# Local block: the inverse roots for q and k made by VectorE with a product of two quadratics, in place of ten small operations of GpSimd

## What is computed

```python
def l2norm(t):
    return t / jnp.maximum(jnp.linalg.norm(t, axis=-1, keepdims=True), 1e-12)

def attn_layer(x, Wqkv, qs, ksc, Wo):          # 16 heads of 64, window of 32
    q, k, v = jnp.split(x @ Wqkv, 3, -1)       # then by heads
    q = l2norm(q) * qs
    k = l2norm(k) * ksc
    q = q * cos * scale + rotate_half(q) * sin * scale
    k = k * cos / scale + rotate_half(k) * sin / scale
    return local_attention(q, k, v) @ Wo

for i in range(6):
    x = attn_layer(shift_tokens(x), ...) + x
    x = ffn_layer(shift_tokens(x), ...) + x
```

## Time and profile before

| | before |
|---|---|
| median of 3 runs | 4272.27 us (4267.4 to 4280.25) |
| profiled execution | 4279.95 us, span 4278.2 us |
| mean granted TensorE clock | 0.971 |
| TensorE (PE) busy | 3950.0 us, 92% |
| weight loads (PEld) busy | 2888.7 us, 68% |
| VectorE (DVE) busy | 3287.6 us, 77% |
| ScalarE (ACT) busy | 2637.3 us, 62% |
| GpSimd (POOL) busy | 2977.4 us, 70% |

### The profile page before, as it was taken

The page is one execution under the profiler, slowest core; times in us unless marked ns, Lnnn a source line. Parts: engine busy times, 40 slices in busy tenths (PEclk is TensorE's granted clock), DMA queues, the critical chain, the costliest instruction groups (busy, mean ns, idle before and its releaser), DMA issues. The chain is left out here.

```text
span 4278.2 us, 151283 instructions
## 1 busy us (share of the span) xinstructions
PE 3950.0 (92%) x66376; PEld 2888.7 (68%) x66376; DVE 3287.6 (77%) x4155; ACT 2637.3 (62%) x3184; POOL 2977.4 (70%) x3649
## 2 busy tenths in 40 slices
PE   8999969999999999999878887799999999999997
PEld 5655657777777777777633333577777777777775
DVE  4535568888888888888668884688888888888885
ACT  4424436667767666666537774367667767667664
POOL 2202158889888888888634440788888988888884
PEclk9999989999999999999979998899999999999998
DMA  4304332333233323322100000332333333233221
GB/s 152 126 10 141 110 92 79 80 94 84 79 87 86 86 76 87 88 69 73 40 11 1 1 1 1 110 84 78 87 79 86 89 82 89 74 87 84 75 68 37
DMA packets 169727, 316.93 MB, mean 74 GB/s; under 512 B 39336, under 2 KB 43056, under 8 KB 166640
## 3 DMA queue, kind: packets, MB, share of 16 engines
q1 hardware_dynamic: 153520, 241.18, 20.8%
q0 software_dynamic: 15552, 66.07, 5.0%
HBM read 92.03 MB, written 20.05 MB: 26 GB/s over the span
## 5 line engine op out<-in xcount | busy, mean ns | idle before, releaser
L695 PE MATMUL psum<-loc_w_hl,loc_z_lo 128*128 128x512 f32 x1152 | 513.9, 446 | 39.5 <-DMA loc_w_hl<-parted 26.0
L1191 DVE TENSOR_REDUCE loc_ssq<-loc_sq 128x16 f32<-128x1024 f32 x384 | 464.6, 1210 | 24.2 <-POOL loc_rn L1074 24.2
L936 ACT ACTIVATE loc_sq<-psum 128x1024 f32<-128x1024 f32 x192 | 196.5, 1024 | 457.1 <-PE psum L697 452.0
L1078 POOL TENSOR_TENSOR loc_rc_k<-loc_rc_k,loc_rs_k 128x1024 f32<-128x1024 f32 x192 | 454.1, 2365 | 18.7 <-DVE loc_rs_k L1205 18.7
L1078 POOL TENSOR_TENSOR loc_rc_q<-loc_rc_q,loc_rs_q 128x1024 f32<-128x1024 f32 x192 | 459.1, 2391 | 0.0
L696 PE MATMUL psum<-loc_w_hl,loc_z_hi 128*128 128x512 f32 x1152 | 455.8, 396 | 2.1 <-issue 2.1
L1186 DVE TENSOR_TENSOR loc_rc_q<-psum,loc_rot 128x1024 f32<-128x1024 f32 x192 | 235.0, 1224 | 289.1 <-ACT loc_sq L931 159.9
L697 PE MATMUL psum<-loc_w_hl,loc_z_hi 128*128 128x512 f32 x1152 | 455.7, 396 | 0.2 <-issue 0.2
L792 PE MATMUL psum<-loc_PT,loc_V 64*64 64x32 f32 x24576 | 405.1, 220 | 7.3 <-issue 6.7
L792 PEld LDWEIGHTS psum<-loc_PT,loc_V 64*64 64x64 f32 x24576 | 381.2, 135 | 33.7 <-issue 10.1
L1097 POOL TENSOR_TENSOR loc_prob<-loc_prob,loc_recip 128x1024 f32<-128x1024 f32 x192 | 365.4, 1903 | 43.6 <-DVE loc_recip L1228 43.5
(11 more groups left out here) (198 smaller groups left out, 9616.7 us busy)
## 6 DMA issues: line engine op xcount, KB each, us to landing
loc_V<-loc_V SPq DMA_DIRECT2D x1152, 128.0 KB
loc_V<-loc_V SPq DMA_DIRECT2D x672, 64.0 KB
loc_w_hl<-parted POOLq DMA_DIRECT2D x72, 512.0 KB, 4.4
parted<-moe_halves POOLq DMA_DIRECT2D x18, 1024.0 KB, 5.2
moe_spread<-moe_gates SPq DMA_DIRECT2D x64, 256.0 KB, 4.0
moe_raw<-in_wqkv POOLq DMA_DIRECT2D x18, 512.0 KB, 6.3
moe_w<-in_moe_w SPq DMA_DIRECT2D x32, 256.0 KB, 3.3
loc_wo<-in_wo SPq DMA_DIRECT2D x12, 512.0 KB, 5.1
```

The costliest lines, as they stand in the source:

```text
L695: pe.matmul(M.bank[bank + g], z_lo[:, r, tokens], w[:, 0, cols], start=True, stop=False)
L1078: pool.tensor_tensor(rc, rc, rs[:, :], ALU.add).then_inc(added, 1)
L1191: dve.tensor_reduce(ssq[:, a:a + HEADS], heads(sq[:, :]), AX_X, ALU.add).then_inc(totalled, 1)
```

## The change

The function `root` moves from GpSimd's list to VectorE's, behind `guess`, and becomes six operations in five dependent stages: t = g*g*x, with g the guess and x the sum of squares, and then g times the product of two quadratics in t. The leading factor of that product goes into the tables of cosine and sine. The guess goes to a tensor `rg` of its own, so that `rn` is written once. `floored` becomes a `scalar_tensor_tensor` with `ssq` as both inputs.

```diff
+ROOT_LEAD = 0.27406619329149995
+ROOT_FACTORS = ((-0.9034896806386632, 1.7067896912217941), (-4.2420135386446685, 5.265389317482745))
...
-            def root(L, t):
-
-                step = L * (TS * 9) + t * 9
-                pool.wait_ge(guess_ready, upto(L, t))
...
-                pool.tensor_tensor(rn[:, :], rn[:, :], rt[:, :], ALU.mult).then_inc(root_ready, 1)
-
...
             def step(L, n, live):
-                if live(n - 1):
-                    root(L, n - 1)
...
-                dve.tensor_scalar(ssq[:, :], ssq[:, :], 1e-24, None, ALU.max).then_inc(floor_ready, 1)
+                dve.scalar_tensor_tensor(out=ssq[:, :], in0=ssq[:, :], scalar=1e-24, in1=ssq[:, :], op0=ALU.max,
+                                         op1=ALU.max).then_inc(floor_ready, 1)
...
-                dve.tensor_scalar(rn[:, :].bitcast(I32), ssq[:, :].bitcast(I32), -0.5, float(0x5F3759DF), ALU.mult,
+                dve.tensor_scalar(rg[:, :].bitcast(I32), ssq[:, :].bitcast(I32), -0.5, float(0x5F3759DF), ALU.mult,
                                   ALU.add).then_inc(guess_ready, 1)
+
+            def root(L, t):
+
+                step = (L * TS + t) * 5
+                (a, b), (c, d) = ROOT_FACTORS
+                dve.wait_ge(guess_ready, upto(L, t))
+                dve.tensor_tensor(rt[:, :], rg[:, :], rg[:, :], ALU.mult).then_inc(root_step, 1)
+                dve.wait_ge(root_step, step + 1)
+                dve.tensor_tensor(rt[:, :], rt[:, :], ssq[:, :], ALU.mult).then_inc(root_step, 1)
+                dve.wait_ge(root_step, step + 2)
+                dve.scalar_tensor_tensor(out=rv[:, :], in0=rt[:, :], scalar=c, in1=rt[:, :], op0=ALU.add,
+                                         op1=ALU.mult).then_inc(root_step, 1)
+                dve.scalar_tensor_tensor(out=ru[:, :], in0=rt[:, :], scalar=a, in1=rt[:, :], op0=ALU.add,
+                                         op1=ALU.mult).then_inc(root_step, 1)
+                dve.wait_ge(root_step, step + 3)
+                dve.scalar_tensor_tensor(out=rv[:, :], in0=rv[:, :], scalar=d, in1=rg[:, :], op0=ALU.add,
+                                         op1=ALU.mult).then_inc(root_step, 1)
+                dve.wait_ge(root_step, step + 5)
+                dve.scalar_tensor_tensor(out=rn[:, :], in0=ru[:, :], scalar=b, in1=rv[:, :], op0=ALU.add,
+                                         op1=ALU.mult).then_inc(root_ready, 1)
...
                 if live(n):
                     floored(L, n)
                     guess(L, n)
+                    root(L, n)
...
-    tab = np.stack(tabs).astype(f)
+    tab = (np.stack(tabs) * ROOT_LEAD).astype(f)
```

More of the change, by code:

```diff
@@ L557, in local_transformer_block @@
         rc_k = sb("rc_k", [P, 2, INNER])
-        ssq, rn, rt, ru = (sb(n, [P, 2 * HEADS]) for n in ("ssq", "rn", "rt", "ru"))
+        ssq, rn, rg, rt, ru, rv = (sb(n, [P, 2 * HEADS]) for n in ("ssq", "rn", "rg", "rt", "ru", "rv"))
         qk_q, qk_k = (sb(n, [P, PAIRS, 2, DH]) for n in ("qk_q", "qk_k"))
```

## The result

The changed kernel takes 4345.12 us (median, 4326.52 to 4353.02) beside 4275.96 us (4267.4 to 4280.25) for the kernel before on the same chip: a ratio of 1.015, 95% interval 1.0123 to 1.0178. The change costs 1.5%, about 65 us. The forecast was 4253 us with a range up to 4315: wrong in its sign, and the time is outside the range.

A forecast was written before the change was run, and what follows sets the result against it. GpSimd's loop was taken as the bound, 63.3 us per four-tile group. New loop: 58.5 + 1.54 + 0.7 + 1.0 + 0.9 + 0.3 = 62.9; 0.4 x 48 = 19 us off the 4272 median gives 4253, range 4195 to 4315.

The forecast's parts named there:

- The stall moves: Local block: a VectorE-GpSimd-VectorE loop of 14.63 us per plain tile replaces GpSimd's; DMA issues fall into its waits, costing nothing.
- sum of 62.9 us per group: New loop over four local-block tiles plus extras, against 63.3 before; TensorE's 60.8 us busy time stays under it.
- rival (c): Nothing happens, 4272 us: small steps eat the 0.4 us, or TensorE and the awaited squares already set the pace; chance 0.24.
- without a hole: VectorE runs from the q sine product to the reciprocal's end with no wait, 9.03 us per tile.
- new loop: Plain local-block tile: VectorE to the reciprocal, GpSimd's normalise and add k, then VectorE's floor, guess and root; 14.63 us.
- The floor: VectorE's small instruction before the guess: held by GpSimd's add k for 1.8 us, mean rising from 886 ns to 1.5 or more.
- rival (b): Faster by more: only tensor_scalar waits for GpSimd, the new instruction forms don't; 72 us gained, 4200 us; chance 0.12.
- The root: Inverse root on VectorE, five dependent stages at 194 ns plus 0.03 each: 1.12 us per tile, bounds 0.9 to 1.25.
- The deviation chain: GpSimd's eight small instructions, every fourth tile: their 1.04 us power catches the third or fourth root step, costing 0.9 us.
- rival (a): Slower: the deviation chain wins shared access at every root step, root 1.2 us later every fourth tile, 4310 us; chance 0.22.
- z_lo: GpSimd instruction slipping in ahead of the guess: guess takes about 1 us every fourth tile, adding 1.0 us per group.
- The reciprocal: GpSimd's normalise waits for VectorE's reciprocal about 2.7 us in nearly every tile, 300 to 500 us in all.

The follow-up runs named there:

- e8: Changed kernel with the weight DMA issue moved behind scale q in GpSimd's list: 4279.42 us, 0.9995 of the kernel before.
- e16: e8 plus six useless 128x32 products on GpSimd behind the root: 4332.58 us, ratio 1.0122 to the kernel before.
- e7: Changed kernel with the weight issue waiting for VectorE's root, plus six useless 128x32 GpSimd products ahead of that issue: 4289.59 us, ratio 1.0024.
- e12: e8 with the six root operations on VectorE left out: 4249.59 us, 0.9931 of the kernel before.
- e10: Changed kernel with the weight issue moved behind normalise, ahead of add k: 4408.83 us, ratio 1.0304 to the kernel before.

## Why the prediction was wrong, and where it was right

**The step that failed** stands under "The stall moves": the DMA issues "fall into the new waits (1.8 us before the floor, 2.7 us before normalise), so they cost nothing while those waits stand". For the 0.6 us of GpSimd's time this is true: in the example the issue at 1511.57 lies in a wait of GpSimd for the root (a third wait, neither of the two named). But I had priced only the instruction, not its transfer, and not that GpSimd's list without the root lets it go 3.7 us earlier. SyncE's queue was never looked at. The price of that step was 66 us (after against e8); its term in the sum was nought. No rival had it.

**The loop was not the bound.** The sum of 62.9 us per group (the additions redone give the same but for 0.1 us of table factors) stood on the claim that "TensorE's 60.8 us stay under 62.9", with idle time left as it was. Without the collision, e8, the waits of TensorE over the stretch are

```profile
PE psum L768 <- issue: 33.8, 26, 2.4
PE psum L794 <- issue: 6.8, 11, 1.3
PE psum L697 <- issue: 4.9, 4, 1.9
PE psum L824 <- DVE loc_gg L1247: 4.8, 8, 0.9
```

The wait for q is gone, 30.5 us, and the waits for issue, all lines together, went from 17.7 us to 48.8. Wait for q and waits for issue together are 48.2 us before and 48.8 in e8: the relief was taken back by TensorE's own stalls, and a group takes 64.4 us there, not 62.9. So the 19 us of forecast gain were not there even with the collision away: 4279 against the 4253 forecast. That is rival (c), by its second reason (TensorE already near its pace); I had given it 0.24. The likely reading is that while TensorE waited for q its instruction supply caught up, and that this wait had hidden the stalls. That is argued from the equal sums; e16, meant to test it, was spoiled by its overlap, and e7 can't test it, for TensorE has no wait for q there. It stays open. TensorE is not the bound alone: leaving six operations off VectorE gave 30 us (e12).

**VectorE "without a hole"** was wrong. The waits of VectorE in the changed kernel, same stretch:

```profile
DVE loc_rc_q L1159 <- ACT loc_sq L933: 105.2, 79, 7.1
```

It waits for ScalarE's square of q in 79 of 80 tiles, 1.3 us on average (70.3 us at 58 places before). ScalarE in turn waits for TensorE's projections, mostly ahead of the square of k, which comes earlier in its list:

```profile
ACT loc_sq L938 <- PE psum L699: 206.9, 79, 6.0
ACT loc_sq L933 <- PE psum L699: 21.8, 22, 2.1
```

So the new loop goes through TensorE too. The prediction had seen that wait and dismissed it, because the floor behind it waited for GpSimd anyway; when that cover went, it should have been put in. It also explains the next point.

**The floor** was to rise from 886 ns to 1.5 us or more. It fell:

```profile
L1169 DVE SCALAR_TENSOR_TENSOR loc_ssq<-loc_ssq 128x32 f32<-128x32 f32 x79 | 43.3, 548 | 4.8 <-DVE loc_ssq L1164 0.5 <-issue 0.2
...
L1183 DVE TENSOR_TENSOR loc_rt<-loc_rg 128x32 f32<-128x32 f32 x79 | 16.1, 204 | 2.7
...
L1185 DVE TENSOR_TENSOR loc_rt<-loc_rt,loc_ssq 128x32 f32<-128x32 f32 x79 | 15.2, 192 | 2.7
```

VectorE comes so late to the floor that add k is often over: over the whole span 110 of 192 floors took under 0.3 us, where there were 40 before. Where it is early, the new form waits just as the old one did, as the prediction said: a floor that took 1.59 us in the changed kernel, while GpSimd's add k ran from 768.50 to 770.87:

```profile
769.33 1.59 DVE L1169 SCALAR_TENSOR_TENSOR loc_ssq<-loc_ssq 128x32 f32<-128x32 f32 x1
```

So rival (b), that the new forms escape, is out. VectorE's busy time rose by 104 us, not by 250 to 400, for the same reason: the root keeps it busy for 193 us (222 by the sum of the steps, two pairs of which overlap), and over the whole span the floor (169.0 to 113.9 us) and the guess (78.3 to 47.8) gave back 86.

**The root** was sized right: steps of 185 to 204 ns against the 194 of the earlier trace rows, about 1.1 us for five stages.

**The deviation chain** was drawn wrong. The prediction let its power catch a root step (0.9 us), rival (a) let it win every step. The timeline of the changed kernel, both engines:

```profile
1597.53 0.26 POOL L1086 TENSOR_SCALAR loc_var<-loc_stats 128x4 f32<-128x4 f32 x1 [0.52 <-DVE loc_stats L1239]
...
1598.28 1.05 POOL L1090 TENSOR_TENSOR loc_rstd<-loc_var,loc_minus_half 128x4 f32<-128x4 f32 x1 [0.19 <-POOL loc_lift L1087]
...
1600.65 0.20 POOL L1101 TENSOR_TENSOR loc_lift<-loc_lift,loc_rstd 128x4 f32<-128x4 f32 x1
1600.80 1.90 POOL L1059 TENSOR_TENSOR loc_qk_k<-loc_rc_k,loc_rn 128x1024 f32<-128x1024 f32 x1
```

```profile
1598.68 0.19 DVE L1195 SCALAR_TENSOR_TENSOR loc_rn<-loc_ru,loc_rv 128x32 f32<-128x32 f32 x1
```

The root steps run beside the chain undisturbed, also beside the power, and the last ends at 1598.87. Scale k starts at 1600.80, because it stands behind the chain in GpSimd's list. The wait is 1.9 us in that tile, where 0.9 was forecast, and for another reason. Over the whole span 133 root steps start while the power runs, and the longest of them takes 0.19 us: the prediction had counted each as exposed to whatever GpSimd runs. z_lo was forecast to show as a guess of about 1 us in every fourth tile, 48 in all. It does so in 8 (1.19 us at most), where there were 41 before: for most of the rest VectorE comes after it.

**The reciprocal** came as drawn. The page's row of the changed kernel:

```profile
L1072 POOL TENSOR_TENSOR loc_prob<-loc_prob,loc_recip 128x1024 f32<-128x1024 f32 x192 | 365.5, 1903 | 564.5 <-DVE loc_recip L1222 564.5
...
L1059 POOL TENSOR_TENSOR loc_qk_k<-loc_rc_k,loc_rn 128x1024 f32<-128x1024 f32 x192 | 365.0, 1901 | 230.4 <-DVE loc_rn L1195 230.2
```

GpSimd waits for it at 190 of 192 tiles, 3.0 us each (2.7 forecast; 564 us in all where 300 to 500 were named), and for the root in most tiles. These two waits come to 795 us, where those at normalise and at the first root step came to 79 before: the work taken from GpSimd is now waiting.

## What to carry to other kernels

When work is taken out of an engine's list, every DMA issue behind it can move forward by as much: find on the other queues what its transfer will now meet, not only where the issuing instruction fits. If a change to arithmetic brings a loss that its arithmetic can't explain, move each DMA issue back alone; here one such move returned 66 us, and the changed kernel then equals the kernel before (0.9975 to 1.0015), though no version that does all the work beat it. And a wait that vanishes from the busiest engine is a gain only if that engine has nothing of its own queued behind it: compare the sum of all its waits, not the one that was removed.

## What the runs showed of the hardware

- TensorE can stop in the middle of a run of independent matmuls, by up to 5.4 us (e10), when 512 KB of weights and the copies of v move at the same time. Such stops are shorter but there without that (33.8 us at the scores line in e8, 2.4 at most).
- All 367 such stops of 1 us and more in the 18 traces ended 1.1 to 1.7 us after the end of a 16 KB transfer of the instruction queue.
- After the stall of 3.38 us the granted clock was 0.50 for some 6 us.
- 133 VectorE steps of 128x32 with both inputs in SBUF started while GpSimd's power of 128x4 ran, and none took over 0.19 us; a floor that started while GpSimd's add k ran took 1.59 us.
- A place of the issue that is harmless in one kernel cost 1.3% in the other: the same place in GpSimd's list, behind scale q, gave an overlap of 19 (4279 us) and of 185 (4335 us).
